# Graph attention and routed experts on one Trainium2 core: the adjacency of the first attention loaded in two column sides, its counting split, Gelu in batches, zero products on TensorE

## What is computed

```python
x = x + gelu(attention0(_layernorm(x), adj) @ Wh)
x = x + experts0(_layernorm(x))            # top 2 of 8 experts
x = x + attention1(_layernorm(x), adj)     # 4 heads
x = x + experts1(_layernorm(x))

def _L0_gnn_ref(X, A, W, r):
    Wh = X @ W.T
    s_i = Wh @ r[:F_out, 0]
    s_j = Wh @ r[F_out:, 0]
    e = s_i[:, None] + s_j[None, :]
    e = jnp.where(e >= 0, e, ALPHA * e)
    e = jnp.where(A == 0, -jnp.inf, e)
    attention = jax.nn.softmax(e, axis=1)
    return jax.nn.gelu(attention @ Wh, approximate=False)
```

## Time and profile before

| | us |
|---|---|
| median of 3 runs | 1987.38 |
| lowest, highest | 1985.22, 1990.87 |
| profiled execution, device time | 1985.19 |
| its span in the profile | 1983.5 |
| PE busy | 1663.3 (84%) |
| DVE, ACT busy | 1000.5, 1030.1 |

### The profile page before, as it was taken

One profiled execution on the slowest core, in us unless ns is written; L12 is line 12 of the kernel. 1 busy time (PEld: TensorE's weight loads), 2 busy tenths in 40 slices (PEclk: granted clock), 3 DMA queues, 4 the chain that ended last, 5 costly groups with the idle time before them and its releaser, 6 DMA issues. The chain is left out here.

```text
span 1983.5 us, 42662 instructions
## 1 busy us (share of the span) xinstructions
PE 1663.3 (84%) x12926; PEld 1536.0 (77%) x12927; DVE 1000.5 (50%) x2248; ACT 1030.1 (52%) x2127; POOL 329.1 (17%) x282
## 2 busy tenths in 40 slices
PE   4639999994679999294997988979965899999998
PEld 3538888883569999174997988979965799999997
DVE  4638888786622222477776776766767011111011
ACT  1634444443335555015877887878842445455453
POOL 1100000000037766000000000000000333333332
PEclk9959999996589999597998999989966899999999
DMA  9960000003357777500000000000044666666664
GB/s 149 108 129 14 8 16 8 21 0 111 111 151 203 202 205 189 167 0 19 11 8 17 16 15 12 13 12 17 8 154 154 211 179 182 183 185 183 176 179 106
DMA packets 81362, 190.01 MB, mean 96 GB/s; under 512 B 9562, under 2 KB 52854, under 8 KB 72470
## 3 DMA queue, kind: packets, MB, share of 16 engines
q1 hardware_dynamic: 48438, 138.73, 21.2%
q0 software_dynamic: 27280, 45.56, 14.3%
q10 hardware_dynamic: 5584, 4.99, 0.8%
HBM read 189.37 MB, written 33.11 MB: 112 GB/s over the span
## 5 line engine op out<-in xcount | busy, mean ns | idle before, releaser
L1256 PE MATMUL bank<-arena 128*128 128x195 bf16 x5408 | 479.1, 250 | 74.5 <-DVE arena L1116 46.6
L1256 PEld LDWEIGHTS bank<-arena 128*128 128x128 fp8e4 x5408 | 469.8, 98 | 83.8 <-issue 81.8
L1021 ACT ACTIVATE arena<-arena,m_row 128x512 fp8e5<-128x512 f32 (+1 forms) x728 | 429.4, 677 | 101.8 <-DVE arena L1116 89.7
L1708 PEld LDWEIGHTS bank<-X,arena 128*128 128x128 f32 x2832 | 338.5, 194 | 5.9
L1708 PE MATMUL bank<-X,arena 128*128 128x128 f32 x2832 | 338.9, 277 | 0.0
L1805 DVE TENSOR_TENSOR arena<-bank,X 128x256 f32<-128x256 f32 x118 | 50.1, 424 | 557.1 <-PE bank L1746 557.1
L1746 PE MATMUL bank<-arena,X 128*128 x1416 | 327.6, 381 | 1.7 <-ACT X L1781 1.7
L884 PE MATMUL bank<-arena 128*128 (+1 forms) x1352 | 300.3, 384 | 15.9 <-DVE arena L827 15.9
L884 PEld LDWEIGHTS bank<-arena 128*128 128x128 f32 x1352 | 257.5, 191 | 57.8 <-issue 21.8
L1746 PEld LDWEIGHTS bank<-arena,X 128*128 128x128 f32 x1416 | 259.8, 190 | 39.0 <-issue 8.4
L805 ACT ACTIVATE bank<-arena,s_all 128x384 f32<-128x384 f32 (+1 forms) x234 | 133.9, 573 | 185.0 <-DVE arena L819 176.5
(11 more groups left out here) (205 smaller groups left out, 1325.8 us busy)
## 6 DMA issues: line engine op xcount, KB each, us to landing
arena<-m1w SPq DMA_DIRECT2D x67, 1024.0 KB, 4.9
arena<-m0w SPq DMA_DIRECT2D x67, 512.0 KB, 4.0
arena<-adjT POOLq DMA_DIRECT2D x26, 416.0 KB, 13.0
xs<-X SPq DMA_DIRECT2D x4, 1664.0 KB, 6.9
arena<-qd SPq DMA_DIRECT2D x25, 256.0 KB, 3.2
xe<-zeros POOLq DMA_DIRECT2D x1, 3456.0 KB, 14.7
X<-x_in SPq DMA_DIRECT2D x2, 1664.0 KB, 11.1
xd<-X SPq DMA_DIRECT2D x13, 256.0 KB, 2.1
```

What stands on the lines that cost most here:

```text
L1021: last = a.activation(self.sign[slot].bitcast(F8W)[:, q * W:q * W + nt * P], self.row[r][:, 0:nt * P], ACT.Sigmoid, scale=STEEP, bias=self ...
L1256: last = pe.matmul(bank[r * NT + n][:, kind * KW:(kind + 1) * KW], self.split[slot][kind].bitcast(F8)[:, q * W + n * P:q * W + (n + 1) * P ...
L1708: last = pe.matmul(bank[2 * s + c // 4][:, c % 4 * P:(c % 4 + 1) * P], self.W1[s][:, k * HID + c * P:k * HID + (c + 1) * P], self.rxt[s][: ...
```

## The change

The mask is now loaded in two column sides: row pairs of the first 12 column tiles (13 loads), then of the other 14 (13 loads), three loads in flight. DVE shifts the mask as it comes, and PE reads its bytes directly as fp8 weights (8 is a positive number in this format), so that the copies to bf16 are gone. Only the first 12 column tiles (group 0) are counted before the attention; column tiles 12 to 20 (group 1) are counted in attention block 1, one row tile after each chunk, into free columns of banks 3 to 5, and tiles 21 to 25 (group 2) in block 3. The two attention blocks of programs are one now. The ring of `prob` has eight slots. The Gelus, additions and layer norm statistics of finished nodes are put between chunks of blocks 4 to 8. PE issues products of zeros: 32 after the attention, 4 ahead of the first layer's routing loop and 32 ahead of the second's, and one per tile in both routing loops. The shifts are gone from `tiles_vector`.

```diff
+IDLE_PRODUCTS = 32
+IN_VALUES = 6
+SIDES = (0, 12, T)
+GROUPS = ((0, 12), (12, 21), (21, T))
 def mask_loads_gpsimd(pool, weights_loaded):
+            def load(k):
+                side, c = k // PAIRS, 2 * (k % PAIRS)
+                a, b = SIDES[side] * P, SIDES[side + 1] * P
+                if k >= 3:
+                    pool.wait_ge(mask_loaded[k % 3], 16 * (k // 3))
+                pool.dma_start(m8[:, c:c + 2, a:b],
+                               adjT[c * P:(c + 2) * P, a:b].rearrange("(c p) n -> p c n", p=P)
+                               ).then_inc(mask_loaded[k % 3], 16)
+        def first_shift(v, k):
+            w = words(MASK_AT, MASK_WORDS).bitcast(U32).rearrange("p (c w) -> p c w", c=T)[
+                :, 2 * k:2 * k + 2, 0:SIDES[1] * P // 4]
+            v.wait_ge(mask_loaded[k % 3], 16 * (k // 3 + 1))
+            v.tensor_scalar(w, w, 3, None, ALU.logical_shift_left).then_inc(mask_ready, 1)
+        def second_shift(v, c):
...
 def values_vector(self, v):
+                for i in range(alone, PAIRS - 1):
+                    for s in range(2):
+                        norm(i + 1, s)
+                        keep(i, s)
+                    first_shift(v, i - alone)
+            def group_count(self, pe, g, c):
+                for n, col in enumerate(self.group_columns(g)):
+                    a = c * NP + (t0 + n) * P
+                    last = pe.matmul(col, mask.bitcast(F8)[:, a:a + P],
+                                     self.above[:, at(c * self.L.B, self.L.B)],
+                                     start=False, stop=False, skip_group_check=True)
+            def single_sync(self, sp):
+                self.group_sync(sp, 0)
+                for b in range(L.blocks + 1):
+                    if b == 4:
+                        self.group_sync(sp, 1)
+                    if b == 7:
+                        self.group_sync(sp, 2)
+                    sp.wait_ge(self.rows_free[r], b // 2 + 1)
+                    sp.dma_start(self.rows[r].rearrange("p (q w) -> p q w", w=L.W)[:, :, 0:w],
+                                 q_all[:, b * L.W:b * L.W + w].partition_broadcast(P)).then_inc(self.rows_loaded[r], 16)
+            RING = 8
 def single_scalar(self, a):
+                block_of(3, self.nt)
+                a.wait_ge(self.banks_free[0], 3)
+                self.gelu_pairs(a, 0, 4)
+                exp_again()
+                block_of(4, self.nt)
+                self.group_scalar(a, 2)
+                for b in range(5, 7):
+                    block_of(b, self.nt)
+                a.wait_ge(self.banks_free[1], 4)
+                self.gelu_pairs(a, 4, 9)
+                exp_again()
+                block_of(7, self.nt)
+                block_of(8, self.L.tail // P)
+                a.wait_ge(self.banks_free[1], 5)
+                self.gelu_pairs(a, 9, 12)
+                a.wait_ge(self.banks_free[0], 6)
+                self.gelu_pairs(a, 12, PAIRS)
 def single_vector(self, v, stat):
+                def block_of(b, nt):
+                    if b == 1:
+                        for k in range(3):
+                            v.wait_ge(mask_loaded[k], 16 * ((2 * PAIRS - 1 - k) // 3 + 1))
+                    larger(b, nt, 0, 0, 0)
+                    for q in range(R):
+                        larger(b, nt, q + 1, (q + 1) % R, (q + 1) // R)
+                        masked(b, nt, q, q, 0)
+                        if b == 1:
+                            second_shift(v, q)
+                        if q == 3 and b > 0:
+                            normalise(b - 1, nt_)
+                    if b in (2, 4):
+                        self.group_rows(v, b // 2)
+                    if b == 5:
+                        add_pairs(0, 4)
+                    if b == 6:
+                        stats_of(0, 4)
+                    if b == 7:
+                        add_pairs(4, 7)
+                    if b == 8:
+                        stats_of(4, 7)
...
+                add_pairs(7, 9)
+                stats_of(7, 9)
+                add_pairs(9, 12)
+                stats_of(9, 12)
+                normalise(L.blocks, L.tail // P)
+                add_pairs(12, PAIRS)
+                stats_of(12, PAIRS)
 def single_tensor(self, pe):
+                        if group is not None:
+                            pe.wait_ge(mask_ready, PAIRS + c + 1)
+                            self.group_count(pe, group, c)
...
+                pe.wait_ge(self.banks_free[1], L.blocks // 2 + 1)
+                with pe.Fori(0, IDLE_PRODUCTS):
+                    pe.matmul(bank[5][:, :], zeros[:, 0:P], zeros[:, :], start=True, stop=True)
 def route_tensor(self, pe):
                     last.then_inc(self.lg_done, 1)
+                    idle_product()
+                with pe.Fori(0, IDLE_PRODUCTS if self.second_norm else 4):
+                    idle_product()
 def tiles_vector(self, v):
-                    if not self.second_norm:
-                        m32 = words(MASK_AT, MASK_WORDS).bitcast(U32)[:, at((i - 1) * size, size)]
-                        v.tensor_scalar(m32, m32, 3, None, ALU.logical_shift_left)
```

336 lines of the change are left out of this document (209 added, 127 removed).

## The result

| | before | after |
|---|---|---|
| median of 13 runs each, us | 1987.68 | 1982.31 |
| lowest and highest, us | 1985.22, 1990.87 | 1980.66, 1986.59 |
| profiled execution, us (span) | 1985.19 (1983.5) | 1982.61 (1980.9) |
| mean granted clock | 0.920 | 0.923 |

The ratio of after to before is 0.9975, 95% interval 0.9967 to 0.9983: 5 us less, small but clear of the interval, and inside the 0.3% that I had called the limit of a measurement here. I had forecast 1940.

What follows compares the result with a forecast made beforehand. Adjacency loading was taken to bound the start, PE the attention, half-clock PE the routing loops. Terms -43.4 + 13.6 + 8 - 16 - 9 = -46.8 gave profiled 1938, median 1940; own range 1926 to 1953, with rivals 1924 to 1966.

Steps and rivals of the forecast that it cites:

- The step that failed is 5: Both routing loops: one zero product per tile keeps PE at full clock, -4.5 us each.
- Rival B: Routing loops: clock is lost and not lifted; 1956 if first layer only (chance 0.17), 1971 if both (0.07).
- Step 1: Start: counting only the first 12 column tiles brings the first exponential to 97.5 instead of 140.92, -43.4 us.
- bounds 0 and 24: Start: limits on the 3 us added for loading the rows beside side two's loads; 24 if behind side two.
- Rival C: Start: the rows' load stands behind side two, block 0 starts at 121 instead of 97.5; 1964, chance 0.07.
- Step 2: Attention blocks 1 and 3: 364 count products cost 13.1 us plus 0.5 for wider clearing, +13.6.
- Rival D: Attention blocks 1 and 3: count products between f32 products do not overlap, 0.193 us each; 1997, chance 0.04.
- Step 3: Attention: work put between chunks stops PE, 6.6 us plus about 1.4 for Gelus and table loads, +8.
- the ring: Attention: eight slots instead of four bring nothing, since chunk 24's slot is slot 0 with either.
- Step 4: Attention's end to routing: first routing product 13.6 us after PE's end, not 29.6, -16.
- Step 6: Experts: removed shifts gain 0, as DVE's 15.4 us there lie beside a full PE.
- Rival E: Attention: block 1 waits for side two, starting late, say by 8 us; 1948, chance 0.05.

Runs made afterwards that it cites:

- e2: Changed kernel with four zero products instead of 32 in the loop ahead of the second routing: 1970.7 us, ratio 0.9916.
- e4: Changed kernel with 12 and 32 zero products written out straight before the gate-weight wait, replacing the loops of 4 and 32 ahead of the routings: 1969.6 us.
- e13: e3 with e7's spread, GpSimd's load pause, later gate wait, straight zero products (16, 12, 46) before the routing loops and two per tile: 1926.9 us.
- e6: e3 with GpSimd holding side two's loads from the fifth on until the first rows are loaded: 1947.8 us, ratio 0.9811.
- e8: e3 with four slots in the ring instead of eight: 1950.5 us, ratio 0.9813.
- e7: e3 with additions and statistics of blocks 5 to 8 spread after every second chunk, none in block 8: 1945.5 us, ratio 0.9789.
- e3: Changed kernel without any of the added zero products: 1952.1 us, ratio to before 0.9820.
- e14: e13 with one zero product per tile instead of two: median 1930.5 us, executions 1917 to 1923 and 1938 to 1940.
- e1: Changed kernel without the zero product after each routing tile, those ahead kept: 1956.9 us, ratio 0.9849.
- e11: e3 with a shift by 0 bits put back into the first layer's experts: 1954.3 us, ratio 0.9837.
- e12: e4 with the one 512-column zero product per tile split into two of 256: 1961.4 us, executions 1952.7 to 1969.6.
- e5: e4 with two zero products of 512 columns per tile instead of one: 1957.3 us, ratio 0.9839.
- e16: e13 without the straight zero products ahead, two per tile kept: 1941.1 us, ratio 0.9789.

## Why the prediction was wrong

**The step that failed is 5.** "That the clock stays up rests on one comparison ... I take it that with them the clock holds." It did not, in either loop (451.5 to 482 and 1454.6 to 1485 at 0.50). The comparison was of a loop of count products at 1.00 with a loop at 0.50, which differ in more than the columns, and it was used to say that one more product makes the second like the first. The count loop itself does not bear it out either: the earlier trace rows have it at 0.80 from 71 to 127, and just behind the ten microseconds that I had picked it stood at 0.50, with the same products:

```profile
105.00:111.70 6.70, 3.13 (x52) 2.82 (x52) 1.84 (x2) 3.27 (x2) 1.91 (x2) 0.50 1.04 108
```

And there was nothing to hold: both loops of the changed kernel began at 0.50, and one product per tile did not raise it. Where a loop did begin at 1.00 with one, it stayed there in three of four profiled cases. The tile was 1.52 us, so each routing cost 8.5 more instead of 4.5 less: 26 us off for the two. (The 4.5 was itself too small: with the tile times of the prediction it is 26 x 0.19 = 4.9, and a tile at full clock with one product took 0.81 us, not 1.0.)

**I left a queue out.** I costed the loop of 32 behind attention and not the one of 32 ahead of the second routing, though both stand in the diff. There the first tile is ready 13 us into the block, and 32 products at 0.62 us take 20: 9.7 us, shown by e2. For the price per product I had "0.21 us each if streamed at full clock, perhaps 0.3 with the branch". In the loop behind attention, at full clock, the first 19 turns took 0.22 us each (in e2 the first 10) and the others 0.38; ahead of the second routing a turn took 0.62 at half clock. Written out, a product took 0.21 (e4) at full clock and 0.43 (e13) at half.

**Rival B was right, and named the right place.** "If it falls and the zero products do not lift it, each costs 0.43": 1971 for both layers, at a chance of 0.07. Measured per tile 0.33. With the 32 products that B did not count either, B gives 1971 - 5 + 10 = 1976. I held it at 0.24 in all against 0.60 because the gap ahead of the first loop looked short, under 3 us; it was 4.6 us from the last weight load of the 32 to the next, and e4 shows that the loop can fall behind a gap of 1.0 us all the same.

**Step 1: right but for one size.** The count ended at 83.6 (forecast 82.7) and the Exp stood at 86.7 (85.8). The store and load of the rows under side two's loads cost 7.1 us more than in the kernel before, where I added 3; "bounds 0 and 24" held it. e6 confirms the cause, loads in flight beside them: without these, 5.3 us in all. Rival C, rows behind all of side two, did not come.

**Step 2: right.** "13.1; 0.5": measured 8.6 + 5.4 = 14.0. Rival D is out: a count product between f32 products costs 14.0/364 = 0.038 us, the wider clearing included. (D would have turned the change slower from 0.036 + 46.8/364 = 0.165 us on; the 0.18 of the prediction holds only with 6 us of noise added.)

**Step 3: right in kind, 2.6 us too high.** 6.6 + 1.4 forecast, 5.4 measured (6.0 less 0.6, block 0 being 0.6 shorter), and the ring brings nothing (e8). e7 adds what I had not asked: the stalls of blocks 5 to 8 came only of the heaping behind the eighth chunk.

**Step 4: right within 1.4 us.** Of the 15.0 us that are left, e3, without zero products, needs 11.7. One reading was wrong: in the trace of before VectorE ended the last chunk 2.2 us ahead of PE's end (453.22, and a wait of 2.26 before L834), not 3.5. The 32 products, longer than that path, covered it.

**Step 6** is open: the first layer's experts took 4.2 us more in the changed kernel and 3.4 to 5.6 more in most variants, but 2.3 in e2, 1.4 in e14 and 1.1 in e8 (246.0 us), which differs from e3 in attention's code alone. Up to there e2 is the changed kernel word for word, and took 1.9 us less, so part of this changes from execution to execution, and each kernel has one profile. Neither the zero products (e1, e3) nor the shifts (e11) cause it; what does stays open. Rival E did not come: side two was loaded when block 1 began.

The times did move as forecast until 451 us: there the changed kernel was 33.4 us ahead. It then gave 26.7 back in the two routings and 4.1 elsewhere. That it ended near the time of before is chance: a gain of 33 us and a loss of 31, most of it in work that was meant to gain.

## What to carry to other kernels

Work that is meant to keep the clock up is real work on an engine that may be the bound; look at what it costs if the clock stays down, and at each place where the first useful instruction waits behind it. Check the granted clock in several executions, not one: in e12 and e14 the same program gave two groups of times, and the mean clock of each execution told which. Look, too, at the level at which a loop is entered before comparing what goes on inside it. Here small pieces of work on a following engine fitted between chunks for nothing when spread, and stopped the leading engine when heaped. A small store and load on the critical path were worth a pause of the bulk loads beside them, as far as these had slack.

## What the runs showed of the chip that I had not expected

- A loop shown busy throughout may be at 1.2 GHz (before, e3), fall from 2.4 GHz with no more than 1.0 us idle at a time in the 5 us before (e4, by 451.5) or climb from 1.2 (e5, e16). More products per tile made the full clock surer and the tile longer at once; two per tile, at 1.02 us, were still shorter than none at 1.17.
- At full clock a routing tile took 0.75 us without and 0.81 with a zero product. My estimate that ScalarE would hold it at 1.0 was too high.
- A one-product loop cost up to 0.17 to 0.19 us per turn beyond the product itself (0.38 against 0.21 at full clock, 0.62 against 0.43 at half), but nothing for its first 19 turns behind attention, 0.22 us each.
- With loads of side two in flight the store and the load of the first rows took 14.6 us together, without them (e6) 5.3.
